# First attention joined in chunks of queries beside its last tiles, with doubled tiles and divided projections, in a two-attention layer on one core

## The chip, the cores and the metric

The kernel runs on one NeuronCore of one Trainium2 chip. The metric is the device time of one execution, in microseconds (us); the median of three runs is what is compared. The profile is one further execution of the same program.

## What is computed

For each of B = 4 sequences of L = 2048 rows of D = 256 values, two attentions follow one another, each with a residual and a layer norm:

```python
# first attention: 16 heads of 16; softmax over m, but the value row is that of the query l
x_proj = (x @ w_in.T + b_in).reshape(b, l, 16, -1);  q, k, v = jnp.split(x_proj, 3, axis=-1)
att = softmax(jnp.einsum('blhd,bmhd->blmh', q, k) * scale, axis=2)
opt = jnp.einsum('blmh,blhd->blhd', att, v).reshape(b, l, d)
x = layernorm(x + opt @ w_out.T + b_out)
# second attention: 4 of 16 heads of 64, chosen by a softmax of the mean of x @ Wr + br
Q, K, V = the chosen heads of x @ Wq + bq, x @ Wk + bk, x @ Wv + bv
O = softmax(Q K^T / 8) V
x = layernorm(x + O @ Wo + bo)
```

## The kernel before

The kernel is one program in which every engine has a list of units of work. A planner, `plan()`, makes the lists when the program is built: it plays the work through with a cost in us for each unit, and writes down in which order each engine took its units. On the chip each engine runs its list strictly in that order and waits on semaphores. So the planner's numbers move no work in time by themselves; they set the order. TensorE (PE) takes the unit with the lowest `spot` among the heads of six hand-made lists (`work_lists()`): `main`, `scores`, `products`, `inputs`, `tiles` and `late`.

The units that matter here, with their names in `plan()`:

- `XT`, `QP`, `KP`, `VP`: transposes of a chunk of 512 rows of x, and its projections to queries, keys and values. `QP` and `KP` take one bank of PSUM each, `VP` two. `LV` splits queries and keys into bf16 levels, `SV` stores them, `LS` loads the levels of one head into `stack`.
- `A`: a tile of the first attention, 128 queries by 1024 keys (two matmuls of 512 columns, two banks). VectorE (DVE) takes the minimum of each row (L1185), ScalarE (ACT) exponentiates and sums (L1003). There are 512 tiles in each sequence: 16 heads by 16 tiles of queries by 2 halves of the keys. PSUM has 8 banks, so at most four tiles are in flight.
- `J`: the halves of the keys are joined. Once all 512 tiles are done, DVE finds the lower minimum for all 16 tiles of queries at once, subtracts (`join_first`), ACT exponentiates, and DVE multiplies, adds, takes the reciprocal and multiplies (`join_second`).
- `AT`, `OT`, `OP`: for each chunk c of 512 queries GpSimd (POOL) scales the value rows (L752), PE transposes them, ACT copies them to `oT`, PE projects them (L830). Then the layer norm: DVE adds the residual and takes the statistics (L1161 to L1171), ACT takes the root (`LN`, L1060 and L1062), and `NM` refines and scales (L712 to L721), on DVE for `OP`.
- `X1`, `RT`, `LW`: the rows are transposed into `x1T` (L838); when all four chunks are there, the routing is worked out on PE, DVE and ACT, and SyncE (SP) loads the weights of the chosen heads.
- `FK`, `FQ`, `FV`: the projections of the second attention (L844, L830). `S`, `T`, `V`: its scores for the maxima (L927, read by DVE L1264), its scores again for the exponentials (L942), and its products (L962). `D`, `R`, `FO`: sums, scaling, output projection and second layer norm.

The sequences overlap: while the second attention of sequence b runs, the tiles `A` of sequence b+1 run between its units. I call the stretch from the last tile `A` of a sequence to the first scores `S` of the same sequence a seam; there are four, and sequence 3 has no tiles of a next one to put into its seam. Before the first seam only sequence 0's tiles run, with all the `inputs` between them (L844, L830 of `fq` and `w_inT`); I call it the first stage. `AHEAD` is the number of tiles of the next sequence that the lists give to a seam.

Of the kernel before, what the change touches and what calls it, by code (L numbers as in the profile page):

```python
# [13 lines left out]
P = 128  # L14
# [3 lines left out]
CH = 512  # L18
# [20 lines left out]
HEAD_TILES = NT * HALF  # L39
RING = 8  # L40
BURST = 4
BURSTS = STEPS // BURST
AHEAD = 20
# [17 lines left out]

def work_lists():
# [4 lines left out]
    main, late, scores, products, inputs, tiles = [], [], [], [], [], []  # L67
# [22 lines left out]
    for b in range(B):  # L90
        if b + 1 < B:
            tiles += place([("A", b + 1, j) for j in range(AHEAD)], b, near)
        first = []
        for c in range(NCH + 2):
            first += [("OT", b, c)] * (c < NCH) + [("OP", b, c - 1)] * (1 <= c <= NCH) + [("X1", b, c - 2)] * (c >= 2)
        first.append(("RT", b))
        first += [("FK", b, 0, c) for c in range(NCH)] + [("FQ", b, 0, 0)]
        main += place(first, b, near)
# [4 lines left out]
    for r in range(B * rounds + behind):  # L103
# [8 lines left out]
        for i, kind in enumerate(spots):  # L112
# [21 lines left out]
            if kind == "V" and at:  # L134
                was = ((at - 1) // GROUPS, (at - 1) % GROUPS)
                main += [(spot, ("D",) + was)] * (step == 4) + [(spot, ("R",) + was)] * (step == 8)
                if at // GROUPS + 1 < B:
                    main += [(spot, ("FO", was[0], was[1] // PAIRS))] * (step == 12 and was[1] % PAIRS == 1)
                else:
                    main += [(spot, ("FO",) + divmod((at - 2) // PAIRS, NCH))] * (step == 2 and at % PAIRS == 1)  # L140
    for b in range(B - 1):
        tiles += [(b + 0.9999, ("A", b + 1, j)) for j in range(given[b], A_TILES)]
    main += [(B + 0.99, ("D", B - 1, GROUPS - 1)), (B + 0.99, ("R", B - 1, GROUPS - 1)), (B + 0.99, ("FO", B - 1, NCH - 1))]
    for units in (late, scores, products, tiles):
        units.sort(key=lambda entry: entry[0])
    main.sort(key=lambda entry: entry[0])
    return [main, scores, products, inputs, tiles, late]


def plan():  # L150
# [9 lines left out]
    def fill(tag, us, banks, after, read_by):  # L160
        name = ("PE",) + tag
        unit(name, us, after)
        banks_of[name], reader[name] = banks, read_by
# [5 lines left out]
    sp = lambda *t: ("SP",) + t  # L169
    jobs = [t for at, t in lists[3] if t[0] == "XT"]  # L170
    norms = []
    for b in range(B):
        norms += [("OP", b, c) for c in range(NCH)] + [("FO", b - 1, NCH - 1)] * (b > 0)
        norms += [("FO", b, c) for c in range(NCH - 1)]
    norms.append(("FO", B - 1, NCH - 1))
# [14 lines left out]
    for i, half in enumerate(halves):  # L190
        for kind, eng in (("QP", dve), ("KP", act)):
            t, two = (kind,) + half, (kind,) + halves[i - 2]
            fill(t, 1.85, 1, [act("XT", half[0], half[2])], eng(*t))
            split = dve if kind == "QP" and half[0] == 0 else pool
            was = dve if kind == "QP" and two[1] == 0 else pool
# [1141 lines left out]
```

## Time and profile before

| | |
|---|---|
| median of 3 runs | 3965.09 us (3962.86 to 3968.43) |
| profiled execution, its own time | 3961.53 us |
| its span | 3959.8 us |
| busy: PE, DVE, ACT, POOL | 90%, 88%, 78%, 41% |
| granted TensorE clock, mean | 0.911 |

The span is the time from the first to the last instruction. A busy share is an average over stages. The granted clock is given as a share of full speed; 1.00 is 2.4 GHz and 0.50 is 1.2 GHz. Views of stretches below show for each engine how long it was busy, and in brackets how many instructions it ran.

### The profile page before, as it was taken

Reading aid. Unit: us, or ns where it says so; the run is one execution under the profiler, and the core shown is the slowest. Engines: PE = TensorE matmul, PEld = TensorE weight load, DVE = VectorE, ACT = ScalarE, POOL = GpSimd, SP = SyncE. Lnnn points to the kernel's source line nnn. Section 1 sums busy time; section 2 is a strip of 40 time slices with the busy share of each in tenths; the row PEclk is TensorE's granted clock in tenths of the full one; section 3 lists DMA queues with packets and bytes.
Section 4 is the critical chain, followed back from the end, with each engine's and each line's share of the span. In section 5 each row is a group of like instructions: output and inputs, shape, how many; then the busy total and the mean of one; then the engine's idle time right before and its main releaser. Section 6 shows DMA issues by size and latency. Waiting matters only on the chain.

```text
span 3959.8 us, 41484 instructions
## 1 busy us (share of the span) xinstructions
PE 3559.1 (90%) x13768; PEld 1260.7 (32%) x13768; DVE 3464.9 (88%) x3484; ACT 3097.4 (78%) x5053; POOL 1624.5 (41%) x1086
## 2 busy tenths in 40 slices
PE   7888888888999999799999999799999999799997
PEld 3233232232223232433322232333323232443333
DVE  7888889979999999879999999879999999667786
ACT  4888888867999999778999999678999999424333
POOL 3122233101444444423444444333444444737675
PEclk7677777679999999899999999799999999899998
DMA  5222222110000000200000000200000000100000
GB/s 161 69 74 71 74 75 73 55 52 17 17 17 27 17 27 17 83 23 12 27 17 27 17 27 16 87 22 17 27 17 27 17 27 1 56 7 12 11 11 11
DMA packets 117192, 142.60 MB, mean 36 GB/s; under 512 B 33394, under 2 KB 100466, under 8 KB 116978
## 3 DMA queue, kind: packets, MB, share of 16 engines
q1 hardware_dynamic: 116978, 139.95, 11.5%
q8 instruction: 110, 1.80, 0.2%
q14 instruction: 104, 0.85, 0.1%
HBM read 89.55 MB, written 50.33 MB: 35 GB/s over the span
## 4 chain that ended last, share of the span: by engine, by line
PE 42%; DVE 39%; ACT 14%; issue 3%; POOL 1%; SPq 1%; DMA 0%; DVEq 0%; POOLq 0%; ACTq 0%
DVE nmax L1185 26%; ACT ps L1003 13%; PE ps L962 10%; DVE smax L1264 9%; PE ps L865 8%; PE ps L830 6%; PE ps L844 6%; PE ps L927 5%; PE ps L942 5%; PE ps L977 1%; PE ps L838 1%; DVE y L721 1%; POOL facc L789 1%; DVE vals L1201 0%; PE ps L945 0%
## 5 line engine op out<-in xcount | busy, mean ns | idle before, releaser
L1003 ACT ACTIVATE ps<-ps,nmax 128x1024 f32<-128x1024 f32 x2048 | 2230.0, 1091 | 302.8 <-DVE nmax L1185 273.5
L1185 DVE TENSOR_REDUCE nmax<-ps 128x1 f32<-128x1024 f32 x2048 | 2382.3, 1215 | 95.3 <-PE ps L865 88.7
L865 PE MATMUL ps<-stack 96*128 96x512 bf16 x4096 | 1342.7, 426 | 206.3 <-ACT ps L1003 122.8
L789 POOL TENSOR_TENSOR facc<-facc,probs 128x1024 f32<-128x1024 f32 x443 | 1041.6, 2351 | 861.0 <-ACT probs L1090 776.4
L865 PEld LDWEIGHTS ps<-stack 96*128 96x128 bf16 x4096 | 280.5, 101 | 1373.9 <-ACT ps L1003 939.7
L1264 DVE TENSOR_REDUCE smax<-ps 128x2 f32<-128x1024 f32 x512 | 619.3, 1215 | 47.1 <-PE ps L927 47.0
L927 PE MATMUL ps<-fk,fq 64*128 64x512 f32 x2048 | 574.5, 644 | 63.1 <-ACT ps L1003 56.8
L942 PE MATMUL ps<-fq,fk 64*128 64x512 f32 x2048 | 548.4, 614 | 10.8 <-DVE probs L1294 5.5
L962 PE MATMUL ps<-probs,vals 128*64 128x512 f32 x2048 | 517.2, 612 | 4.4 <-ACT probs L1090 3.4
L1090 ACT ACTIVATE probs<-ps 128x1024 f32<-128x1024 f32 x384 | 389.2, 1015 | 26.7 <-PE ps L945 26.2
L1003 ACT ACTIVATION_READ_ACCUMULATOR ps<-ps,nmax 128x1 f32 x2048 | 409.0, 200 | 0.0
L1079 ACT ACTIVATE probs<-probs 128x1024 f32<-128x1024 f32 x128 | 135.0, 1056 | 219.3 <-DVE probs L1294 188.4
L942 PEld LDWEIGHTS ps<-fq,fk 64*128 64x128 f32 x2048 | 190.1, 190 | 289.9 <-issue 139.8
L927 PEld LDWEIGHTS ps<-fk,fq 64*128 64x128 f32 x2048 | 165.2, 187 | 301.4 <-ACT ps L1003 201.0
L699 POOL CAST fk<-vals 128x512 bf16<-128x512 f32 x56 | 35.3, 631 | 458.8 <-DVE vals L1191 368.4
L962 PEld LDWEIGHTS ps<-probs,vals 128*64 128x64 f32 x2048 | 116.8, 136 | 267.6 <-issue 205.8
L795 POOL TENSOR_TENSOR oacc<-oacc,part 128x512 f32<-128x512 f32 x72 | 90.8, 1262 | 259.4 <-ACT part L1100 259.4
L1294 DVE TENSOR_TENSOR probs<-ps,stack 128x1024 f32<-128x1024 f32 x128 | 154.7, 1215 | 37.5 <-PE ps L942 28.6
L786 POOL TENSOR_TENSOR facc<-probs 128x1024 f32<-128x1024 f32 x32 | 75.2, 2349 | 266.5 <-ACT probs L1090 227.5
L945 PE MATMUL ps<-frows,minus 64*128 64x512 bf16 x768 | 149.2, 382 | 0.0
L844 PE MATMUL ps<-fq,w_inT 128*128 128x512 f32 x256 | 136.1, 663 | 9.6 <-ACT fq L1009 4.8
L844 PE MATMUL ps<-x1T,wqk_sel 128*128 128x512 f32 x256 | 128.2, 637 | 12.9 <-DMA bqk_sel<-in_L_ffn_bq 10.2
(127 smaller groups left out, 2035.6 us busy)
## 6 DMA issues: line engine op xcount, KB each, us to landing
stack<-qk_levels SPq DMA_DIRECT2D x768, 64.0 KB, 2.2
qk_levels<-fk SPq DMA_DIRECT2D x64, 384.0 KB, 2.6
probs<-in_L_attn_x SPq DMA_DIRECT2D x16, 512.0 KB, 3.8
res<-in_L_attn_x SPq DMA_DIRECT2D x16, 512.0 KB, 4.4
v_rows<-vals SPq DMA_DIRECT2D x16, 512.0 KB, 2.6
vrows<-v_rows SPq DMA_DIRECT2D x16, 512.0 KB, 3.4
x_rows<-y SPq DMA_DIRECT2D x16, 512.0 KB, 2.9
res<-x_rows SPq DMA_DIRECT2D x16, 512.0 KB, 3.8
```

The lines of the kernel that those rows point to most:

```text
L789: pool.tensor_tensor(total, total, probs[:, slot, :], ALU.add).then_inc(facc_ready, 1)
L830: last = pe.matmul(ps[:, banks[t // 2], (t % 2) * D:(t % 2 + 1) * D], rowsT[:, cc, t * P:(t + 1) * P], w[:, cc, :], start=(cc == 0), stop= ...
L844: last = pe.matmul(bank(banks[0]), wT(cc), columns(cc), start=(cc == 0), stop=(cc == KC - 1))
L865: last = pe.matmul(bank(banks[i]), stack[0:SK, hd % 2, 0, t * P:(t + 1) * P], stack[0:SK, hd % 2, 1, col:col + CH], start=True, stop=True)
L927: last = pe.matmul(bank(banks[h]), fq[rows, pair, qs:qs + P], fk[rows, pair, ks:ks + CH], start=True, stop=True)
L942: last = pe.matmul(bank(banks[h]), fk[rows, pair, s * P:(s + 1) * P], fq[rows, pair, c * CH:(c + 1) * CH], start=True, stop=b + 1 == B)
L962: last = pe.matmul(ps[rows, into, :], vals[:, s, (2 * pair + h) * FD:(2 * pair + h + 1) * FD], probs[:, slot_of(b, g, s), h * CH:(h + 1) * ...
L1003: act.activation(src, src, ACT.Exp, bias=nmax[:, b % 2, half, t, hd:hd + 1], scale=-1.0, accum_out=esum[:, b % 2, half, t, hd:hd + 1]).the ...
L1090: act.activation(probs[:, slot_of(b, g, s), :].rearrange("p (h n) -> p h n", h=2), two_banks(banks), ACT.Exp, scale=float(FD) ** -0.5).the ...
L1185: dve.tensor_reduce(nmax[:, b % 2, half, t, hd:hd + 1], two_banks(banks), AX.XY, ALU.min).then_inc(min_ready, 1)
L1264: dve.tensor_reduce(smax[:, g % 2, s // NCH, :, s % NCH], two_banks(banks), AX.X, ALU.max).then_inc(smax_ready, 1)
L1294: dve.tensor_tensor(probs[:, slot_of(b, g, s), :].rearrange("p (h n) -> p h n", h=2), two_banks(banks), bc[:, g % 2, :].rearrange("p (h n) ...
```

## The change

1. **Joining by chunks.** `CHUNK_LAST` names the last tile of each chunk of 512 queries in the last head (every 8th of its 32 tiles). For each chunk, as soon as its tiles are done, DVE takes the lower minimum (128x64), POOL subtracts (128x128), ACT exponentiates, POOL multiplies and adds, DVE takes the reciprocal, and POOL multiplies before it scales the value rows. `nmax` and `att` hold the values, no longer `oT`. A new list `seam` holds `OT`, `OP`, `X1`, `RT` and the first `FK` and `FQ`, with spots from the tiles of their chunks.
2. **Layer norm.** `NM` of `OP` goes to POOL for the first three chunks (`nm`), and stays on DVE for the last. The order of the norms changes with it.
3. **`AHEAD`** is 32 in place of 20.
4. **Divided projections** (`PARTS`): `QP`, `KP`, `FK`, `FQ` and `D` are issued in two pieces, `VP`, `FV`, `OP` and `FO` in four, and other units can come between the pieces. The banks are held from the first piece. By `PATIENT` a tile goes ahead of such a piece when the planner has nothing queued on DVE.
5. **Doubled tiles** (`again`): where the planner has work queued on DVE and none of the last 12 PE units was `S`, `T`, `BC` or `V`, the two matmuls of a tile are issued twice, with the same operands into the same banks. 324 of the 512 tiles of sequence 0 are doubled, and 17, 15 and 15 of the others.
6. **Splitting.** `LV` of the queries of sequence 0's second half of heads goes from DVE to POOL (4 of 8 on DVE go).
7. **Planner.** The cost of `A` on PE is 0.47 in place of 0.437, of `A` and `S` on DVE 1.165 in place of 1.135. Units in `URGENT` go first on an engine.

```diff
+CHUNK_LAST = [A_TILES - HEAD_TILES + (c + 1) * TPC * HALF - 1 for c in range(NCH)]
-AHEAD = 20
+AHEAD = 32
+PARTS = {"QP": 2, "KP": 2, "FK": 2, "FQ": 2, "VP": 4, "FV": 4, "OP": 4, "FO": 4, "D": 2}
+URGENT = ("J", "AT", "OT", "OP", "X1", "RT")
+PATIENT = {k: 20 for k in ("QP", "KP", "VP", "XT", "FK", "FQ", "FV", "OP", "FO", "OT", "X1", "D", "R", "RT")}
+NEAR = 12
...
+    nm = lambda k, b, c: ((dve if k == "OP" and c + 1 == NCH or k == "FO" and b + 1 == B else pool)("NM", k, b, c))
...
-        unit(dve("J", b, 0), 1.2, [act("A", b, A_TILES - 1)] + ([pe("FO", b - 2, NCH - 1)] if b >= 2 else []))
-        unit(act("J", b), 0.63, [dve("J", b, 0)])
-        unit(dve("J", b, 1), 4.2, [act("J", b)])
         for c in range(NCH):
-            unit(pool("AT", b, c), 1.95, [dve("J", b, 1), sp("LV", b, c)])
+            unit(dve("J", b, c, 0), 0.6, [act("A", b, CHUNK_LAST[c])] + ([pool("AT", b - 1, c)] if b else []))
+            unit(pool("J", b, c, 0), 0.4, [dve("J", b, c, 0)])
+            unit(act("J", b, c), 0.4, [pool("J", b, c, 0)])
+            unit(pool("J", b, c, 1), 0.6, [act("J", b, c)])
+            unit(dve("J", b, c, 1), 0.5, [pool("J", b, c, 1)])
+            unit(pool("AT", b, c), 2.2, [dve("J", b, c, 1), sp("LV", b, c)])
...
+            kind = best and best[2][3 if best[2][1] == "part" else 1]
+            if not queued and kind in PATIENT and at[4] < len(tiles):
+                spot, t = tiles[at[4]]
+                if pe(*t) in pe_ready and pick(2) and spot < best[0] + PATIENT[kind] / A_TILES:
+                    best = (spot, 4, pe(*t))
...
+                twice = n[1] == "A" and queued and not any(m[1] in mode for m in order["PE"][-NEAR:])
+                if twice:
+                    again.add(n)
...
+                elif kind == "J":
+                    b, c, later = at
+                    both, whole = of_chunk(c, nmax[:, b % 2, :, :, :]), chunk_att(c)
+                    base = (b * NCH + c) * COMB_STEPS
+                    if later == 0:
+                        pool.wait_ge(lowest, b * NCH + c + 1)
+                        pool.tensor_tensor(both, whole.unsqueeze(1).to_broadcast([P, HALF, TPC * AH]), both,
+                                           ALU.subtract).then_inc(comb, 1)
+                    else:
+                        pool.wait_ge(comb_e, b * NCH + c + 1)
+                        pool.tensor_tensor(both, both, of_chunk(c, esum[:, b % 2, :, :, :]), ALU.mult).then_inc(comb, 1)
+                        pool.wait_ge(comb, base + 2)
+                        pool.tensor_tensor(whole, both[:, 0, :], both[:, 1, :], ALU.add).then_inc(comb, 1)
...
-                    for i in range(2):
+                    for i in (0, 1, 0, 1) if n in again else (0, 1):
```

The first place is PE in the middle of the first stage, where the chunks of sequence 1 are projected; `stack` marks matmuls of tiles, `w_inT,fq` the value projection `VP`, `fq,w_inT` the query and key projections, `ident,probs` the transposes `XT`. Before:

```order
L865 MATMUL ps<-stack 128x512 x34
L830 MATMUL ps<-w_inT,fq 128x256 x8
L865 MATMUL ps<-stack 128x512 x10
L838 MATMUL ps<-ident,probs 128x128 x8
L865 MATMUL ps<-stack 128x512 x12
L844 MATMUL ps<-fq,w_inT 128x512 x2
```

The same place in the changed kernel:

```order
L932 MATMUL ps<-stack 128x512 x46
L892 MATMUL ps<-w_inT,fq 128x256 x4
L932 MATMUL ps<-stack 128x512 x4
L892 MATMUL ps<-w_inT,fq 128x256 x2
L932 MATMUL ps<-stack 128x512 x2
L892 MATMUL ps<-w_inT,fq 128x256 x2
L932 MATMUL ps<-stack 128x512 x6
L901 MATMUL ps<-ident,probs 128x128 x8
```

The value projection stood in one piece and now has two and then one tile between its pieces, and the run of tiles ahead of it has more matmuls because most of its tiles are doubled.

The second place is DVE at the end of sequence 1's tiles. `nmax<-ps` are its minima of tiles, `smax` those of the second attention's scores, and `oT` holds the joined values. Before:

```order
L1132 TENSOR_TENSOR oT<-nmax 128x256
L1134 TENSOR_TENSOR oT<-oT,nmax 128x512
L1264 TENSOR_REDUCE smax<-ps 128x2
L1141 TENSOR_TENSOR oT<-oT,esum 128x512
L1143 TENSOR_TENSOR oT<-oT 128x256
L1145 RECIPROCAL oT<-oT 128x256
L1148 TENSOR_TENSOR att<-oT 128x256
```

In the changed kernel the first two chunks there:

```order
L1258 TENSOR_TENSOR att<-nmax 128x64
L1231 TENSOR_REDUCE nmax<-ps 128x1 x2
L1320 TENSOR_REDUCE smax<-ps 128x2
L1231 TENSOR_REDUCE nmax<-ps 128x1 x2
L1261 RECIPROCAL nmax<-att 128x64
L1231 TENSOR_REDUCE nmax<-ps 128x1 x6
L1258 TENSOR_TENSOR att<-nmax 128x64
L1231 TENSOR_REDUCE nmax<-ps 128x1
L1320 TENSOR_REDUCE smax<-ps 128x2
L1231 TENSOR_REDUCE nmax<-ps 128x1
L1261 RECIPROCAL nmax<-att 128x64
L1231 TENSOR_REDUCE nmax<-ps 128x1 x4
```

DVE's six instructions on all the queries have become two small ones for each chunk, with 3 to 5 minima between them, in which POOL and ACT must have done their parts.

The third place is POOL at the last chunk of sequence 1; `facc` are the running sums of the second attention, `newt`, `rstd` and `y` are `NM`, `res` is the residual with its bias, `vrows` is `AT`. Before, POOL's part of the whole join was:

```order
L789 TENSOR_TENSOR facc<-facc,probs 128x1024 x4
L752 TENSOR_TENSOR vrows<-vrows,att 128x1024 x4
L771 CAST flevels<-fmax 128x8
```

In the changed kernel, for the last chunk:

```order
L796 TENSOR_TENSOR nmax<-att,nmax 128x2x64
L848 TENSOR_TENSOR facc<-facc,probs 128x1024
L800 TENSOR_TENSOR nmax<-nmax,esum 128x2x64
L802 TENSOR_TENSOR att<-nmax 128x64
L749 TENSOR_TENSOR newt<-rstd 128x4
L751 TENSOR_TENSOR newt<-newt,var 128x4
L753 TENSOR_SCALAR newt<-newt 128x4
L755 TENSOR_TENSOR rstd<-rstd,newt 128x4
L758 TENSOR_SCALAR y<-y,mv,rstd 128x256 x4
L818 TENSOR_TENSOR res<-res,b_out_rows 128x1024
L807 TENSOR_TENSOR att<-att,nmax 128x64
L811 TENSOR_TENSOR vrows<-vrows,att 128x1024
```

One `facc` addition stands between the two parts of the join, and the scaling of another chunk's norm and a residual stand between the join and `AT`.

## Rows read from the trace of the kernel before

**Rows 1.** The page: span, and each engine's busy time

```profile
span 3959.8 us, 41484 instructions
PE 3559.1 (90%) x13768; PEld 1260.7 (32%) x13768; DVE 3464.9 (88%) x3484; ACT 3097.4 (78%) x5053; POOL 1624.5 (41%) x1086
```

**Rows 2.** Stages: length, busy time of each engine, granted clock, DMA share, GB/s

```profile
59.00:757.00 698.00, 603.00 (x1547) 192.91 (x1546) 624.00 (x559) 601.32 (x1064) 174.81 (x200) 0.71 0.22 72
757.00:957.00 200.00, 158.45 (x535) 70.03 (x534) 163.63 (x210) 134.06 (x233) 24.49 (x15) 0.81 0.15 46
957.00:1606.00 649.00, 606.76 (x2528) 185.91 (x2529) 620.59 (x570) 603.26 (x989) 282.16 (x169) 0.98 0.07 20
1606.00:1806.00 200.00, 168.77 (x670) 75.92 (x668) 156.68 (x207) 139.49 (x231) 73.02 (x47) 0.88 0.17 52
2484.00:2684.00 200.00, 167.88 (x668) 75.21 (x664) 157.49 (x207) 139.49 (x232) 72.76 (x47) 0.89 0.17 51
3367.00:3478.00 111.00, 86.96 (x384) 46.65 (x382) 59.77 (x106) 48.94 (x72) 73.01 (x44) 0.86 0.19 56
3478.00:3960.00 482.00, 451.47 (x1964) 183.95 (x1960) 358.10 (x379) 168.43 (x176) 295.99 (x167) 0.97 0.03 9
```

**Rows 3.** DVE's waits in the first stage: us in total, times, longest

```profile
DVE vals L1201 <- PE ps L830: 44.5, 14, 4.4
DVE vals L1191 <- PE ps L844: 19.5, 20, 2.3
```

**Rows 4.** Timeline of the first stage: start, length, engine, line, count

```profile
400.39 3.72 PE L844 MATMUL ps<-fq,w_inT 128*128 128x512 f32 x4
...
406.96 1.88 PE L844 MATMUL ps<-fq,w_inT 128*128 128x512 f32 x4
...
739.62 18.18 DVE L1185 TENSOR_REDUCE nmax<-ps 128x1 f32<-128x1024 f32 x16
```

**Rows 5.** A 10 us window of the first stage, columns as in rows 2

```profile
730.00:740.00 10.00, 9.13 (x19) 1.18 (x18) 10.00 (x10) 10.00 (x19) 0.00 (x0) 0.50 0.00 0
```

**Rows 6.** DVE's timeline in the seam of sequence 1, idle time ahead in brackets

```profile
1606.28 2.27 DVE L1132 TENSOR_TENSOR oT<-nmax 128x256 f32<-128x256 f32 x1
...
1613.08 2.52 DVE L1143 TENSOR_TENSOR oT<-oT 128x256 f32<-128x256 f32 x1
...
1617.42 0.42 DVE L1148 TENSOR_TENSOR att<-oT 128x256 f32<-128x256 f32 x1
...
1639.01 3.42 DVE L721 TENSOR_SCALAR y<-y,mv,rstd 128x256 f32<-128x256 f32 x4
...
1704.87 0.75 DVE L1246 TENSOR_SCALAR fq<-ps,bqk_sel 128x512 f32<-128x512 f32 x1 [10.20 <-PE ps L844]
...
1707.80 1.22 DVE L1264 TENSOR_REDUCE smax<-ps 128x2 f32<-128x1024 f32 x1
```

**Rows 7.** The same seam until the first scores, and after, columns as in rows 2

```profile
1606.00:1708.00 102.00, 75.38 (x276) 40.15 (x272) 78.89 (x138) 65.22 (x114) 33.87 (x25) 0.77 0.28 87
1708.00:1806.00 98.00, 93.39 (x396) 35.78 (x396) 77.79 (x70) 74.27 (x118) 39.14 (x22) 1.00 0.06 15
```

**Rows 8.** Minima of tiles alone in that seam: DVE busy, clock, DMA, GB/s

```profile
1606.00:1708.00 102.00, 37.22 (x32) 0.77 0.28 87
```

**Rows 9.** The chain through that seam: start, length, what ran

```profile
1694.48 10.35 PE ps L844 x20
...
1705.05 0.86 PE ps L865 x4
```

**Rows 10.** Groups by shape: busy us, mean ns, idle ahead

```profile
L721 POOL TENSOR_SCALAR y<-y,mv,rstd 128x256 f32<-128x256 f32 x48 | 58.0, 1221 | 1.3
...
L721 DVE TENSOR_SCALAR y<-y,mv,rstd 128x256 f32<-128x256 f32 x80 | 42.4, 593 | 0.7
...
L1164 DVE BATCH_NORM_STATS2 st<-y 128x6 f32<-128x256 f32 x128 | 45.0, 414 | 1.1
...
L752 POOL TENSOR_TENSOR vrows<-vrows,att 128x1024 f32<-128x1024 f32 x16 | 30.4, 1932 | 82.1 <-DVE att L1148 82.1
```

More of the change, by code:

```diff
@@ L142, in work_lists @@
         tiles += [(b + 0.9999, ("A", b + 1, j)) for j in range(given[b], A_TILES)]
+    spot_a = {t[1:]: spot for spot, t in tiles}
+    for b in range(B):
+        done = [spot_a[b, j] for j in CHUNK_LAST]
+        seam += [(done[c], (kind, b, c)) for c, kind in ((0, "OT"), (0, "OP"), (0, "X1"), (1, "OT"), (1, "OP"))]
+        seam += [(done[c], (kind, b, c)) for c, kind in ((2, "OT"), (2, "OP"), (1, "X1"))]
+        rest = [("OT", b, 3), ("OP", b, 3), ("X1", b, 2), ("X1", b, 3), ("RT", b)]
+        rest += [("FK", b, 0, c) for c in range(NCH)] + [("FQ", b, 0, 0)]
+        seam += place(rest, max(b, done[3]), near)
     main += [(B + 0.99, ("D", B - 1, GROUPS - 1)), (B + 0.99, ("R", B - 1, GROUPS - 1)), (B + 0.99, ("FO", B - 1, NCH - 1))]
-    for units in (late, scores, products, tiles):
+    for units in (main, late, scores, products, tiles):
         units.sort(key=lambda entry: entry[0])
-    main.sort(key=lambda entry: entry[0])
-    return [main, scores, products, inputs, tiles, late]
+    for units in (main, late, inputs, seam):
+        whole, units[:] = list(units), []
+        for spot, t in whole:
+            parts = PARTS.get(t[0], 1)
+            units += [(spot + i * GAP / A_TILES, ("part", i) + t if i + 1 < parts else t) for i in range(parts)]
+    return [main, scores, products, inputs, tiles, late, seam]
 def plan():
@@ L160, in fill @@
     def fill(tag, us, banks, after, read_by):
-        name = ("PE",) + tag
-        unit(name, us, after)
-        banks_of[name], reader[name] = banks, read_by
+        parts = PARTS.get(tag[0], 1)
+        for i in range(parts):
+            name = ("PE",) + (("part", i) if i + 1 < parts else ()) + tag
+            unit(name, us / parts, after if i == 0 else [])
+            banks_of[name] = banks if i == 0 else 0
+            if i == 0:
+                reader[name] = read_by
     pe = lambda *t: ("PE",) + t
@@ L332, in arrive @@
         else:
-            ready[n[0]].append((now, rank[n], n))
+            ready[n[0]].append((n[1] not in URGENT and n[2] != "OP", now, rank[n], n))
             queued += n[0] == "DVE"
@@ L369, in plan @@
                     held[n] = pick(banks_of[n])
+                    held[n[:1] + n[3:] if n[1] == "part" else n] = held[n]
                     free.difference_update(held[n])
@@ L530, in build @@
         NEWTON_STEPS = 4
-        COMB_STEPS = 6
+        COMB_STEPS = 3
         ROUTE_STEPS = 11
         QK_DMAS, V_DMAS = 4 * FH // PAIRS, 2 * FH
-        order, held, freed, planned = plan()
-        fill_no = {n[1:]: i + 1 for i, n in enumerate(n for n in order["PE"] if n in held and n[1] != "V")}
+        order, held, freed, again, planned = plan()
+        fill_no = {n[1:]: i + 1 for i, n in enumerate(n for n in order["PE"] if n in held and n[1] not in ("V", "part"))}
         nth = {}
@@ L824, in _, with pieces, project_rows @@
             pe.wait_ge(wT_read, 3)
-            def project_rows(banks, rowsT, w):
-                for t in range(TPC):
+            def pieces(kind, piece, count):
+                parts = PARTS.get(kind, 1)
+                return range(count * piece // parts, count * (piece + 1) // parts)
+            def project_rows(kind, piece, banks, rowsT, w):
+                for t in pieces(kind, piece, TPC):
                     for cc in range(KC):
@@ L973, in _ @@
                             shares = (g % 2,)
-                        for t in range(TPC):
+                        for t in pieces(kind, piece, TPC):
                             for h in range(2):
```

143 lines of the change are left out of this document (71 added, 72 removed).

## The prediction

> **What bounds the kernel now.** I read the page's busy shares first [rows 1]: PE 90%, DVE 88%, ACT 78% of the span. No engine is full, so the question is where DVE and PE stand idle. The stages tell it [rows 2]. Between two seams (957 to 1606 us) DVE is busy 620.6 of 649 us and PE 606.8 at a clock of 0.98: nothing is to be had there but less work. The idle time lies in three places. In the first stage (59 to 757) DVE is busy 624.0 of 698.0, 74.0 idle, at a clock of 0.71. In the seams and what follows them it is idle 36.4, 43.3 and 42.5 us of 200 each (the seam of sequence 1 stands for 0 and 2, which differ little), and in the last seam (3367 to 3478) PE, which bounds everything after it, is idle 24.0 of 111.0. The last stage (3478 to 3960) is PE's: 451.5 of 482.0. There the change alters nothing that I price.
>
> Why DVE idles in the first stage is in its waits [rows 3]: 44.5 us for the value projection, 14 times, and 19.5 us for query projections, 20 times: 64.0 of the 74.0. The timeline shows why it is so long [rows 4]: the four matmuls of a projection take 3.72 us where the clock is low and 1.88 where it is high. A tile costs DVE 18.18 / 16 = 1.136 us, so the at most three tiles that wait in PSUM feed it for 3.4 us; a value projection is twice as long as a query projection and outlasts them. Tiles alone leave the clock at its lower level: 0.50, with DVE at 10.00 of 10.00 [rows 5]. So a low clock costs nothing by itself there, only at the projections.
>
> **The change part by part.**
>
> *Divided projections, first stage.* A quarter of a value projection is about 1.9 us at the low clock (3.72 / 2), half a query projection the same, and two tiles then come between pieces. That is under the 3.4 us in PSUM, so the waits should mostly go. But the first two pieces often stand together (the first place shown), 3.7 us. Bounds: 20 us, if only a third of the waits goes, and 64, all of them. I take three quarters, 48.
>
> *Doubled tiles, first stage.* A tile's two matmuls take 0.43 us at the high clock (0.86 for four [rows 9]), a doubled tile 0.86: under 1.136, so DVE sees nothing. At half the clock a doubled tile takes 1.72 and PE paces DVE: 0.58 lost for each. A single tile at the low clock (0.86) costs nothing. The gain of doubling is only that the projections meet a high clock, which the dividing has already made harmless. No row shows what the clock does under doubled tiles. It stood at 0.98 between the seams, where tiles and the second attention share PE [rows 2], and at 0.50 in the tiles alone [rows 5]; doubled tiles are nearer to the former in what they give PE to do. I charge a few dips, 14 tiles' worth: 8 us. Bounds 0 and 324 x 0.58 = 188. First stage: 48 - 8 = **40**. The splitting moved to POOL goes from before the first tile, while PE and the load of the stack are awaited too: nothing, at most 2.
>
> *The seam of sequence 1.* From 1606 to the first scores at 1707.8 it takes 102 us, in which DVE is busy 78.9 [rows 6, 7], 37.2 of it with 32 tiles of the next sequence [rows 8]. In the changed order 42 such tiles stand there: 42 x 1.136 = 47.7. Of the other 41.7 us these go: the join, 10.4 by rows 6 and its neighbours (12 us until 1617.84, less one score reduction of 1.2); three scalings of 4 x 593 ns [rows 10], 7.1; and the statistics of two norms, which now come before the last tile, 4 x 414 ns and an addition of 1.2 each, 5.7. What comes: two small join instructions, each under the 0.42 of L1148 [rows 6], 0.8, and two more score reductions, 2.4. So 41.7 - 10.4 - 7.1 - 5.7 + 0.8 + 2.4 = 21.7, with the tiles 69.4 us for DVE.
>
> Is the chain that short? Before, the join takes 12 us, then 77 us pass for four chunks, routing and loads until PE starts the projections at 1694.5 [rows 9], then 10.4, and 3 to the scores. Now only the last chunk is left. For POOL it is small join instructions (by L752's rate 0.24 for 128x128; I take 0.4 each with their start, 1.6), one scaling of another chunk ahead of `AT`, 4 x 1.22 = 4.9 [rows 10], an addition and a residual of at least 1.9 each, and `AT` 1.9: about 12, no less than the old join. Then one chunk, routing and loads, for which I take 45 of the 77, and projections with tiles between, 15: 72. With the hops in which each step queues behind a tile I take 78 for the seam.
>
> The gain, with tiles counted as work that leaves another stage: before 102 - 37.2 = 64.8; now 78 - 47.7 = 30.3, and 5.7 for the work moved ahead of the last tile (5.7 + three chunks' join 2.4 - the reductions moved in 2.4): 64.8 - 30.3 - 5.7 = 28.8. After the first scores DVE idles another 20.2 of 98.0 us beside PE at 93.4 [rows 7]; the divided `FV` and `FK` give back perhaps 4, since PE has only 4.6 to give. Against it stand two new waits. DVE's `J` minimum has two inputs in SBUF; such instructions took 2.27 and 2.52 us where L1148 took 0.42 [rows 6], beside POOL's additions: up to 2.1 for each of four chunks; I take 3 in all. And DVE's reciprocal of each chunk waits for a round trip over POOL, ACT and POOL; behind it, strictly in order, stand the minima of tiles, for which ACT and then PE wait. Only 3 to 5 minima cover it (3.4 to 5.7 us), and on POOL an addition of sums stands between the two join parts. I take 0.8 a chunk, 3 in all. The 15 doubled tiles cost PE 15 x 0.43 = 6.5 where it is idle anyway: 1. So 28.8 + 4 - 3 - 3 - 1 = 25.8, **26** for each of three seams, **78**. On SP the loads of the next head's stack keep their place behind the weights, except in the first seam, where one load of 12 goes ahead of them while the chain is elsewhere: nothing. Bounds for a seam: 0, and all its idle time, 36.4, 43.3 and 42.5, 122 in all.
>
> *The last seam.* No tiles fill it, so the chain sets it and PE's idle time can go: 24.0, and some at the clock of 0.86. Bounds 0 and 31; I take **18**, since the same two waits stand here.
>
> A rule speaks to the moved scaling. The row: 1221 ns on POOL against 593 on DVE, the latter with its waits in it [rows 10]. The Trainium skill, GPSIMD Engine Reference, Engine selection, says that work with one input runs on GpSimd at roughly line rate. By it the scaling ahead of `AT` would take 2.4 instead of 4.9 us, and the sum would be 2.5 larger for each of four seams, 10 us; the trace decides for the longer.
>
> **The sum.** 40 + 78 + 18 = 136. The profiled execution took 3961.5, which lies 3.6 below the median of 3965.1. 3961.5 - 136 = 3825.5; with the 3.6, **3829 us**.
>
> **The rivals.**
>
> *The seams close wholly* (0.15). DVE's order holds enough tiles, and the idle time of all stages goes: 60 + 110 + 28 = 198, so 3767. For it: 69.4 us of work against 102. Against it: PE follows the seam at 93.4 of 98.
>
> *The seams are no shorter* (0.12). POOL's list is the mechanism: its join parts stand behind additions of sums that wait for ACT's exponentials, and `AT` of the last chunk behind a residual's load. Then each seam gives 3 and the last none: 40 + 9 = 49, 3916. For it: POOL 33.9 of 102 busy leaves room, but strictly in order. Against: three of four chunks are out of the chain in any case.
>
> *The doubled tiles keep PE at the low clock* (0.07), the other side. Its place is the first stage; its price 0.58 for each doubled tile that runs at 0.50. Above (136 + 8) / 0.58 = 248 of 324 such tiles, the kernel is slower: with all, 188, it comes to 3829 - 8 + 188 = 4009. Half of them: 3915. For it: tiles alone fell to 0.50 [rows 5]. Against: PE would then have no gap at all, and the last stage, where it is busy nearly throughout, had 0.97 [rows 2].
>
> *The change does nothing* (0.03): DVE sets the time, the clock stays, 3965.
>
> My forecast has the rest, 0.63, with its own range from 3790 to 3875: the first stage between 20 and 64, a seam between 15 and 38.
>
> **How the numbers follow.** The range from 3772 to 3900 takes the forecast's, and the upper part of the seams that close, and leaves out most of the last three rivals, about 0.2. A measurement here can tell 0.2% (8 us) from no change. Faster: 0.63 + 0.15 + 0.12 and part of the clock's case, 0.91; same 0.03; slower 0.06.
>
> **What would show it.** The first stage should be about 658 us long and DVE's waits for L892 and L907 under 20 us; the clock there above 0.85 if doubling works, and near 0.6 with PE at 100% if it does not. From the last tile to the first scores of sequences 0 to 2 about 78 us with some 42 to 50 tiles in them; in the last seam about 90 of 111. DVE's reciprocal should wait under 1 us on average. I am wrong if the first stage grows, if DVE's idle time in the seams goes to the reciprocals' waits, or if the stages between the seams, which I leave alone, grow by what the seams lose, since PE there is at 93%.

## The result and the profile after

The changed kernel takes 3876.62 us (median of 4 runs, 3868.99 to 3883.73) against 3966.09 us for the kernel before (4 runs). The ratio is 0.9777 with a 95% interval from 0.9764 to 0.9790: 89 us, or 2.2%, less. The forecast was 3829 us, 136 less, with a range from 3772 to 3900. The profiled execution took 3876.35 us.

The page of the changed kernel, span, busy time and granted clock by slices:

```profile
span 3874.3 us, 43074 instructions
...
PE 3551.2 (92%) x14510; PEld 1298.5 (34%) x14510; DVE 3414.4 (88%) x3380; ACT 3102.1 (80%) x5065; POOL 1729.0 (45%) x1262
...
PEclk9999999899999999899999999899999999999998
```

Its stages, cut at the end of a sequence's last tile and at its first scores; [rows 2] and [rows 7] are cut within 3 us of the same events of the kernel before. They are in order: the first stage; the seam of sequence 0; the stage up to the last tile of sequence 1; the seam of sequence 1, the 100 us after it and the rest up to the last tile of sequence 2; the whole from one last tile to the next, which I call a period; the last seam; the last stage.

```profile
57.40:703.70 646.30, 589.27 (x2231) 226.34 (x2230) 623.34 (x567) 602.30 (x1069) 200.83 (x233) 0.99 0.25 81
703.70:792.30 88.60, 73.98 (x258) 32.85 (x258) 74.62 (x108) 76.86 (x141) 23.86 (x26) 0.83 0.28 81
892.30:1552.50 660.20, 608.81 (x2528) 194.89 (x2528) 620.37 (x580) 594.94 (x973) 299.26 (x191) 0.97 0.08 22
1552.50:1637.40 84.90, 77.74 (x308) 38.20 (x309) 68.48 (x103) 70.93 (x126) 39.38 (x43) 0.85 0.29 85
1637.40:1737.40 100.00, 96.69 (x413) 36.67 (x410) 84.50 (x75) 80.93 (x130) 39.93 (x23) 1.00 0.03 8
1737.40:2426.20 688.80, 634.44 (x2649) 208.11 (x2647) 646.11 (x609) 615.57 (x1005) 314.64 (x204) 0.98 0.08 24
1552.50:2426.20 873.70, 808.87 (x3364) 282.98 (x3364) 799.10 (x786) 767.43 (x1259) 393.95 (x269) 0.97 0.10 28
3300.00:3388.10 88.10, 74.79 (x336) 35.41 (x336) 28.07 (x61) 43.06 (x62) 71.50 (x58) 0.93 0.18 53
3388.10:3874.30 486.20, 459.29 (x1980) 183.12 (x1976) 356.69 (x379) 169.17 (x177) 304.97 (x171) 0.97 0.03 9
```

The same period of the kernel before, and its part from 100 us after the first scores:

```profile
1603.70:2481.20 877.50, 801.46 (x3334) 276.72 (x3332) 803.53 (x808) 765.44 (x1256) 371.49 (x229) 0.97 0.10 28
1807.80:2481.20 673.40, 628.73 (x2646) 199.41 (x2648) 643.06 (x600) 622.35 (x1020) 297.22 (x181) 0.99 0.07 21
```

The reader is to see where the 89 us are. All times in this paragraph are between the same two events. The first stage, from the first tile's minimum to the last tile, went from 695.4 us (59.0 to 754.4) to 646.3, its clock from 0.71 to 0.99, and DVE is idle 23.0 us of it. The seam of sequence 1 went from 104 us (1603.7 to 1707.8) to 85, and the last from 115 (3364.1 to 3478.8) to 88. But this period is only 3.8 us shorter: what the seam and the 100 us after it gave, the rest took back, 688.8 us where it was 673.4. DVE's idle time in it is 74.6 us, where it was 74.0. In the kernel before this rest held some 430 tiles by the trace, now 417, so it grew although work had left it. The period before it went from 849.3 to 848.8 us and the one after it from 882.9 to 873.8. The three seams at the head of these periods are 52 us shorter in all, the periods 13: a quarter.

DVE's waits in such a period, kernel before (us in total, times, the longest):

```profile
DVE nmax L1185 <- PE ps L865: 27.6, 61, 3.8
DVE fq L1246 <- PE ps L844: 13.2, 7, 10.2
```

and the changed kernel:

```profile
DVE nmax L1231 <- PE ps L932: 56.7, 100, 3.2
DVE smax L1320 <- PE ps L994: 8.4, 17, 1.0
```

The long wait of the seam (10.2 us for a query projection) is gone; in its place 39 more tiles come late, 29 us in all.

### The profile page after: what moved, and what is told of

Read it like the earlier page. It is cut to its first block, busy times and chain, and to the rows that moved or that the text cites. A ratio compares the mean times of both kernels' runs of the same rounds, so it can differ in the third digit from the quotient of the medians.

```text
span 3874.3 us, 43074 instructions
## 1 busy us (share of the span) xinstructions
PE 3551.2 (92%) x14510; PEld 1298.5 (34%) x14510; DVE 3414.4 (88%) x3380; ACT 3102.1 (80%) x5065; POOL 1729.0 (45%) x1262
## 4 chain that ended last, share of the span: by engine, by line
PE 44%; DVE 33%; ACT 17%; issue 5%; POOL 1%; DMA 0%; SPq 0%; DVEq 0%; POOLq 0%; ACTq 0%
DVE nmax L1231 21%; ACT ps L1071 14%; PE ps L1029 10%; PE ps L932 9%; DVE smax L1320 7%; PE ps L994 7%; PE ps L1009 7%; PE ps L892 5%; PE ps L907 4%; PE ps L1044 1%; PE ps L1012 1%; DVE st L1208 1%; PE ps L901 1%; ACT part L1171 1%; ACT probs L1161 1%
## 5 line engine op out<-in xcount | busy, mean ns | idle before, releaser
L932 PE MATMUL ps<-stack 96*128 96x512 bf16 x4838 | 1369.4, 391 | 192.4 <-ACT ps L1071 104.3
L932 PEld LDWEIGHTS ps<-stack 96*128 96x128 bf16 x4838 | 355.7, 99 | 1324.0 <-ACT ps L1071 757.8
L1009 PE MATMUL ps<-fq,fk 64*128 64x512 f32 x2048 | 557.7, 624 | 16.4 <-DVE probs L1350 5.4
L1071 ACT ACTIVATION_READ_ACCUMULATOR ps<-ps,nmax 128x1 f32 x2048 | 421.4, 206 | 0.0
L736 POOL CAST fk<-vals 128x512 bf16<-128x512 f32 x60 | 37.6, 627 | 393.7 <-DVE vals L1237 346.5
L1350 DVE TENSOR_TENSOR probs<-ps,stack 128x1024 f32<-128x1024 f32 x128 | 154.6, 1216 | 39.5 <-PE ps L1009 20.2
L907 PE MATMUL ps<-x1T,wqk_sel 128*128 128x512 f32 x256 | 132.7, 618 | 6.7 <-DMA bqk_sel<-in_L_ffn_bq 3.6
L907 PE MATMUL ps<-fq,w_inT 128*128 128x512 f32 x256 | 128.7, 614 | 6.7 <-ACT fq L1077 4.8
```

The source lines that it names most:

```text
L907: last = pe.matmul(bank(banks[0]), wT(cc), columns(cc), start=(cc == 0), stop=(cc == KC - 1))
L932: last = pe.matmul(bank(banks[i]), stack[0:SK, hd % 2, 0, t * P:(t + 1) * P], stack[0:SK, hd % 2, 1, col:col + CH], start=True, stop=True)
L1009: last = pe.matmul(bank(banks[h]), fk[rows, pair, s * P:(s + 1) * P], fq[rows, pair, c * CH:(c + 1) * CH], start=True, stop=b + 1 == B)
L1071: act.activation(src, src, ACT.Exp, bias=nmax[:, b % 2, half, t, hd:hd + 1], scale=-1.0, accum_out=esum[:, b % 2, half, t, hd:hd + 1]).the ...
```

## The experiments

All kernels are variants of the changed kernel, whose ratio is 0.9777. Times of the first stage come from one profiled execution each.

**Join at the end.**

```diff
-CHUNK_LAST = [A_TILES - HEAD_TILES + (c + 1) * TPC * HALF - 1 for c in range(NCH)]
+CHUNK_LAST = [A_TILES - 1] * NCH
...
-unit(dve("J", b, c, 0), 0.6, [act("A", b, CHUNK_LAST[c])] + ([pool("AT", b - 1, c)] if b else []))
+unit(dve("J", b, c, 0), 0.6, [act("A", b, CHUNK_LAST[c])] + ([pool("AT", b - 1, c)] if b else []) + ([dve("J", b, c - 1, 1)] if c else []))
```

The order of the norms is the old one here.

> The changed kernel with one part undone: all four chunks' joins wait for the sequence's last tile and follow one another, so no chunk's join, transposes or projections stand ahead of it; doubling, dividing and POOL's share stay. Theory A (the join by chunks is worth what I gave it, and other edits take some of it back in the stages between the seams): it loses what the seams gave, 3 x 26 + 18, so 95 to 100 us more than the changed kernel, a ratio to the kernel before near 1.002. Theory B (the stretch between two last tiles is bound by what PE and DVE have to do in all of it, and a shorter seam only moves idle time): it loses 3 x 4 and some 20 in the last seam, 30 to 40 us, a ratio near 0.986.

3908.12 us, ratio 0.9866 (0.9843 to 0.9890): by the ratios 35 us more than the changed kernel, the sum that theory B had. Its seam of sequence 1, the period that it begins, and its last sequence from the last tile to the end:

```profile
1533.80:1651.00 117.20, 97.46 (x391) 47.30 (x390) 97.02 (x142) 94.08 (x165) 59.56 (x67) 0.85 0.28 84
1533.80:2417.50 883.70, 812.54 (x3372) 285.45 (x3370) 798.87 (x786) 767.56 (x1258) 394.39 (x268) 0.96 0.10 28
...
3298.30:3909.70 611.40, 549.70 (x2363) 228.65 (x2361) 407.55 (x467) 220.78 (x254) 396.39 (x252) 0.94 0.06 18
```

Joining by chunks shortens this seam by 117.2 - 84.9 = 32 us and this period by 10. The next period is 7 us shorter for it, 873.8 and 880.8. But the one before is 12 longer, 848.8 and 836.7, and so is the first stage by 8, 646.3 and 638.5, since with the join at the end no chunk's projections stand ahead of the last tile. Up to the last tile of sequence 3 the two kernels take the same time (3300.0 and 3298.3 us). All of the 35 us comes behind that tile, where no tiles follow: 611.4 - 574.3 = 37. So theory B's sum came, but not its parts. Nor is this the join of the kernel before: here four joins follow one another over DVE, POOL and ACT, and the last seam takes 127.5 us where the kernel before had 114.7. Against the kernel before, the time behind the last tile is 21 us shorter.

**The two remedies of the first stage, one and both undone.** Single tiles:

```diff
-twice = n[1] == "A" and queued and not any(m[1] in mode for m in order["PE"][-NEAR:])
+twice = False
```

> The changed kernel without doubled tiles (371 of them single again), all else as changed. By my prediction the dividing alone makes a low clock harmless: the clock of the first stage falls back to 0.6 to 0.8, the stage stays at 646 us or is up to 8 us shorter, ratio 0.976 to 0.978. Rival (what the first stage gained comes from the clock that the doubled tiles hold up): the first stage is 20 to 40 us longer, ratio 0.983 to 0.988.

Whole input projections (`QP`, `KP` and `VP` left out of `PARTS`):

```diff
-PARTS = {"QP": 2, "KP": 2, "FK": 2, "FQ": 2, "VP": 4, "FV": 4, "OP": 4, "FO": 4, "D": 2}
+PARTS = {"FK": 2, "FQ": 2, "FV": 4, "OP": 4, "FO": 4, "D": 2}
```

> The changed kernel with the input projections (query, key, value of the first attention) in one piece again, the tiles doubled. If the doubled tiles hold the clock up, a value projection takes half as long as before and lasts about as long as the three waiting tiles feed DVE: the first stage loses 5 to 15 us of its 49, ratio 0.979 to 0.982. Rival (only short pieces free DVE): it loses 30 or more, ratio above 0.985.

and both edits together:

> The changed kernel with the input projections whole and all tiles single: both remedies of the first stage undone, the rest as changed. Both theories: the first stage goes back to about 695 us, ratio 0.989 to 0.991, clock there 0.6 to 0.8. Beside the two kernels that lack one of them it tells how far the two overlap.

| kernel | median, us | ratio (95%) | first stage, us |
|---|---|---|---|
| changed | 3876.62 | 0.9777 (0.9764 to 0.9790) | 646.3 |
| whole inputs | 3904.76 | 0.9864 (0.9835 to 0.9893) | 672.5 |
| single tiles | 3950.57 (10 runs) | 0.9972 (0.9961 to 0.9984) | 698.4 |
| both undone | 3987.01 | 1.0070 (1.0043 to 1.0096) | 735.5 |

The first stage with single tiles, at a clock of 0.76:

```profile
57.00:755.00 698.00, 584.95 (x1579) 195.97 (x1578) 622.96 (x566) 602.65 (x1069) 200.99 (x234) 0.76 0.24 74
```

and with doubled tiles and whole inputs, at 0.99:

```profile
58.00:731.00 673.00, 593.76 (x2250) 229.65 (x2248) 624.20 (x567) 606.11 (x1071) 200.89 (x233) 0.99 0.24 77
```

Times the ratios' differences by 3966, doubling is worth 77 us with divided inputs and 82 with whole ones, dividing 34 and 39. They add up; neither makes the other harmless. The first stages alone show less of it, 52 and 63 us for doubling, 26 and 37 for dividing. The profiled executions of two of these kernels were the fastest of theirs, 3933.96 us with single tiles and 3893.19 with whole inputs, so those two stages may be short by some us. With single tiles my theory failed, and the rival was right in its direction and too small (20 to 40 us). With whole inputs the ratio is the rival's, the stage's 26 us lie between the two. With both undone the stage is 40 us longer than both theories had it. The place that shows why, at a value projection, in the kernel with single tiles; PE, then DVE:

```profile
411.46 7.60 PE L932 MATMUL ps<-stack 96*128 96x512 bf16 x14 [0.49 <-ACT ps L1071]
419.12 3.78 PE L892 MATMUL ps<-w_inT,fq 128*128 128x256 f32 x8
422.70 1.91 PE L932 MATMUL ps<-stack 96*128 96x512 bf16 x4
...
423.80 3.48 DVE L1231 TENSOR_REDUCE nmax<-ps 128x1 f32<-128x1024 f32 x3 [2.76 <-PE ps L932]
```

and the same place in the changed kernel:

```profile
382.87 12.57 PE L932 MATMUL ps<-stack 96*128 96x512 bf16 x46 [0.32 <-ACT ps L1071]
395.49 1.99 PE L892 MATMUL ps<-w_inT,fq 128*128 128x256 f32 x8
397.32 1.03 PE L932 MATMUL ps<-stack 96*128 96x512 bf16 x4
...
397.95 3.49 DVE L1231 TENSOR_REDUCE nmax<-ps 128x1 f32<-128x1024 f32 x3 [0.55 <-PE ps L932]
```

A tile matmul takes 7.60 / 14 = 0.54 us in the one and 12.57 / 46 = 0.27 in the other. Two quarters of the value projection that stand together, with two tiles behind them, take 5.7 us at the low clock and 3.0 at the high one, and three minima cover 3.4. The granted clock was 0.53 in the one (419 to 425 us) and 1.00 in the other (395 to 399). DVE waits 2.76 us and 0.55. Over the whole first stage DVE waits 74.0 us in the kernel with single tiles:

```profile
DVE nmax L1231 <- PE ps L932: 44.5, 30, 2.9
DVE vals L1237 <- PE ps L907: 29.5, 12, 2.6
```

In the changed kernel it waits 22.2 (shown further below). The difference, 51.8 us, is the 52.1 us between the two stages.

**The rule that puts tiles first, and the planner's costs.** Single tiles again; first without the rule of `PATIENT` in the first stage, then with whole inputs too:

```diff
-if not queued and kind in PATIENT and at[4] < len(tiles):
+if not queued and kind in PATIENT and at[4] < len(tiles) and tiles[at[4]][1][1] > 0:
```

> The changed kernel with all tiles single, input projections divided, and in the first stage without the planner's rule that lets a tile go ahead of a projection whose place has come while nothing queues for DVE. Single tiles with that rule gave a first stage of 698 us. Theory A (the rule bunches projections and banks, and spoils what dividing gains at a low clock): the first stage comes to 650 to 665 us, as my sum had it for dividing alone, ratio 0.983 to 0.988. Theory B (at a low clock PE has no room for pieces between tiles, rule or not): 690 to 710 us, ratio 0.996 to 1.000.

> As the run before this one, but with the input projections whole too: single tiles, whole input projections, no such rule in the first stage, so that this stage differs from the kernel before only by POOL's share of the splitting and the planner's costs. Theory A (the rule made the undone first stage 40 us longer than before): about 695 us, ratio 0.994 to 0.997. Theory B (the costs or POOL's share did it): 725 to 740, ratio 1.003 to 1.008.

The first came to 3941.12 us, ratio 0.9930 (0.9913 to 0.9946), its first stage to 726.5; the second to 3974.38 us (10 runs), 1.0016 (1.0002 to 1.0029), its first stage to 749.9. So the rule did not lengthen the first stage: without it this stage is 28 and 14 us longer in the profiled executions, and the later stages are shorter by 25 and 12. The medians are 9 and 13 us lower, by the ratios 17 and 21: with single tiles the kernel does better without the rule. Theory A fell both times, and both stages were longer than theory B's too (up to 710 and 740 us). The costs were next, on top of the second of these kernels:

```diff
-fill(("A", b, j), 0.47, 2, ...
+fill(("A", b, j), 0.437, 2, ...
-unit(dve("A", b, j), 1.165, ...
+unit(dve("A", b, j), 1.135, ...
-unit(dve("S", *t), 1.165, ...
+unit(dve("S", *t), 1.135, ...
```

> Single tiles, whole input projections, no tile-first rule in the first stage, as in the run whose first stage took 749.9 us, and now the planner's old costs of tiles too. They put the projections of the first stage back into the close order of the kernel before (one value projection, then QP, 2 tiles, KP, 1 tile, QP, 2 tiles, KP, 17 tiles, where the new costs have 6, 1, 10 and 5 tiles between them). Theory A (that order was worth the 54 us by which the undone first stage is longer than before's): 690 to 705 us, ratio 0.988 to 0.991. Theory B (the splitting moved to POOL or the engines' new order of urgency did it): above 735, ratio 0.999 or more.

3933.89 us, 0.9902 (0.9876 to 0.9928): 45 us less by the ratios, of which the first stage gave 32 (717.4). The ratio is theory A's; the stage lies between the two theories. The new costs spread the projections, and with single tiles that is dear. This stage is still 22 us longer than in the kernel before, but the period behind it is 23 us shorter (825.9 and 849.3). So work of the chunks has moved ahead of the last tile; the seam behind that tile is 78 us long, where it was 103. That this is all of the 22 us is not shown: POOL's share of the splitting is in all these kernels and was not tried alone.

The same costs in the changed kernel, with doubled tiles:

> The changed kernel with the planner's costs of tiles and score reductions as before (0.437 and 1.135 instead of 0.47 and 1.165); the program is otherwise the same. If the costs made the stages between the seams longer (DVE's idle time there 42.6 us instead of 30.3), each gets 8 to 12 us shorter, ratio 0.968 to 0.972. Rival (they only shuffle the order): within 5 us in all, ratio 0.976 to 0.979.

3871.97 us, 0.9759 (0.9742 to 0.9776): the first stage 638.2, the period 870.6, 3 less than with the new costs. The median is 5 us below the changed kernel's, and the two intervals overlap. The costs are not what lengthened the stages between the seams; this is the rival's result. The change has one more part that its list does not name: `D`, `R` and `FO` stand at steps 3, 6 and 9 of a group, where they stood at 4, 8 and 12. With `D` and `R` at steps 4 and 8 as well:

```diff
-(step == 3) + [(spot, ("R",) + was)] * (step == 6)
+(step == 4) + [(spot, ("R",) + was)] * (step == 8)
```

> The changed kernel with the planner's old costs of tiles and score reductions, as in the run that came out 5 us faster than the changed kernel, and with D and R back at steps 4 and 8 of a group. If the earlier steps 3 and 6 are part of what the stages between the seams lost, a period gets 3 to 8 us shorter than with the old costs alone, ratio 0.968 to 0.973, and it is the fastest of all; rival (they cost nothing): 0.975 to 0.977, as with the old costs alone.

3867.84 us (3859.23 to 3882.84), 0.9736 (0.9711 to 0.9761). Its profiled execution was the slowest of its four, with a period of 877.3, so the profile doesn't show the gain that I expected there. It is the fastest median of the kernels that leave nothing out, some 9 us below the changed kernel. Its interval overlaps that of the old costs alone, so neither the theory nor its rival is shown.

**Whole pieces in the seam and between.** `FK`, `FQ`, `FV`, `FO` and `D` in one piece:

```diff
-PARTS = {"QP": 2, "KP": 2, "FK": 2, "FQ": 2, "VP": 4, "FV": 4, "OP": 4, "FO": 4, "D": 2}
+PARTS = {"QP": 2, "KP": 2, "VP": 4, "OP": 4}
```

> The changed kernel with the second attention's projections and denominators (FK, FQ, FV, FO, D) in one piece again; the inputs and OP stay divided. If the pieces, which hold their banks from the first to the last with tiles between, make tiles late in the stages between the seams (DVE waits for them 56.7 us in a period instead of 27.6), those stages get 8 to 12 us shorter and the seams some 4 longer, ratio 0.970 to 0.974. Rival (whole pieces cost DVE more than the banks do): the periods grow by 5 to 15 us each, ratio 0.981 to 0.989.

3884.78 us, 0.9790 (0.9770 to 0.9810), 5 us more, with the two intervals overlapping. Its period is 88.6 + 100 + 684.9 = 873.5, the changed kernel's 873.7. Neither theory holds. In the whole kernel DVE waits 33.2 us for `FV` and 68.6 for the output projections, and 7.3 and 45.1 where they are divided, but the time does not follow these waits. On the other side, its DVE has 8 us less work in this period (790.97), so two effects may cancel here. That the banks held by the pieces cost nothing is not shown.

**What bounds a period.** DVE lightened (the score maxima over half the columns), then PE (three quarters of the score columns):

```diff
-dve.tensor_reduce(smax[...], two_banks(banks), AX.X,
+dve.tensor_reduce(smax[...], two_banks(banks)[:, :, 0:CH // 2], AX.X,
```

> The changed kernel with DVE's work lightened between the seams, to see what bounds it there: the row maxima of the second attention's scores are taken over half the columns only (that part of the computation is left out), about 0.55 us less for each of 128 reductions of a sequence, 70 us of the 874 from one last tile to the next; PE's work is untouched. If DVE paces these stages, a period gets 60 us or more shorter; if PE does, under 15; if both share it, as DVE's idle time that stayed at 74 us a period suggests, 25 to 45. The last sequence's stage is PE's and does not move. Ratio 0.93 if DVE's, 0.967 or more if PE's, 0.945 to 0.96 if shared.

```diff
-last = pe.matmul(bank(banks[h]), fq[rows, pair, qs:qs + P], fk[rows, pair, ks:ks + CH],
+last = pe.matmul(bank(banks[h])[:, 0:3 * P], fq[rows, pair, qs:qs + P], fk[rows, pair, ks:ks + 3 * P],
```

> The mirror of the run before: the score matmuls of the second attention write 384 of 512 columns (the rest is left out), a quarter of the 306 us that they take of PE in a period, some 75; DVE's work is untouched. If PE paces the stages between the seams, a period gets 60 us shorter or more, if DVE does, under 15, and if both share it 25 to 45. The last stage gets 50 to 75 shorter in any case. Should the granted clock in these stages fall with PE's work (it stands at 0.97), the gain says less, and I read it with the clock. Ratio 0.915 if PE's, 0.955 if DVE's, near 0.935 if shared.

3820.02 us, 0.9624 (0.9601 to 0.9646), and 3851.61 us, 0.9705 (0.9682 to 0.9728). Groups of the changed kernel in 800 us between seams (mean ns behind the busy us):

```profile
L1320 DVE TENSOR_REDUCE smax<-ps 128x2 f32<-128x1024 f32 x121 | 146.9, 1216 | 8.7 <-PE ps L994 8.4
...
L994 PE MATMUL ps<-fk,fq 64*128 64x512 f32 x486 | 139.9, 653 | 10.8 <-ACT ps L1071 8.9 <-DVE smax L1320 1.5 <-DVE fq L1302 0.3
```

The group with light DVE, and then that kernel's period:

```profile
L1320 DVE TENSOR_REDUCE smax<-ps 128x2 f32<-128x512 f32 x125 | 85.1, 684 | 15.8 <-PE ps L994 15.7
```

```profile
1532.20:2388.70 856.50, 798.46 (x3362) 276.75 (x3361) 734.69 (x785) 763.71 (x1259) 393.90 (x269) 0.98 0.10 29
```

The group with light PE, and then that kernel's period:

```profile
L994 PE MATMUL ps<-fk,fq 64*128 64x384 f32 x496 | 116.0, 545 | 11.6 <-ACT ps L1071 9.7 <-DVE smax L1320 1.5 <-DVE fq L1302 0.3
```

```profile
1547.90:2418.50 870.60, 788.44 (x3363) 281.90 (x3363) 797.14 (x785) 768.20 (x1259) 394.17 (x269) 0.97 0.10 28
```

128 maxima, each 0.53 us shorter, are 68 us of DVE's time; the period gets 17.2 shorter, a quarter of it (the other two 22.0 and 13.7). That is less than the 25 of a shared bound and more than the 15 of a bound by PE. The run with light PE is a smaller test than I meant. I had counted on 75 us less for PE, from durations that overlap; its busy time falls by 20.4 us, and the period by 3.1, about a sixth (the other two 4.4 and 3.3). The last stage, from which I expected 50 to 75, gave 15 (470.8 for 486.2). Had either engine paced the period alone, its 68 or 20 us would have come out whole; neither did. The clock, 0.97 and 0.98, did not interfere. ACT is busy 767.43 of 873.70 us and is the engine that gives tiles their banks back; I have not lightened it, so what takes the rest is open.

## Why the prediction was partly right

The forecast was 136 us less, and 89 came. The time, 3876.62 us, lies in the range up to 3900, but just above the range from 3790 to 3875 that the forecast had for itself. The direction was right and the first stage and the last seam gave near what was said, the former by luck; the 78 us for three seams were 13.

**The first stage.** I gave it 40 us and it gave some 49, but the step that I built it on failed: "The gain of doubling is only that the projections meet a high clock, which the dividing has already made harmless". Doubling gives 52 us of the first stage (77 of the kernel) and not -8, dividing 26 of the stage with doubled tiles and 37 with single ones (34 and 39 of the kernel), and not 48. That the two sum to more than the stage gained is the third error: I put the planner's new costs at nothing, without a reason, and with single tiles and whole inputs they cost 45 us, with the changed kernel's remedies 5. The term was right in size by errors that cancel, which is luck. What I overlooked stood in my own text: two quarters often stand together, 3.7 us at the low clock, and the tile behind them takes another 0.9 before DVE gets it. I had the number and compared 3.7 with 3.4 as if the excess were all. That "a low clock costs nothing by itself there" fits the tiles alone [rows 5]; the first pieces after them pay, and the tile behind these. The signs named were met: clock above 0.85 (0.99), waits for projections under 20 us (8.2 for L907, none listed for L892). In the changed kernel's first stage:

```profile
DVE nmax L1231 <- PE ps L932: 14.0, 28, 1.2
DVE vals L1237 <- PE ps L907: 8.2, 12, 0.7
```

The rival of a low clock under doubled tiles is refuted; the stage's clock is 0.99.

**The seams of sequences 0 to 2.** The signs inside the seam came near what I said: 78 us forecast, 84.9 measured (88.6 and 85.0 the other two), 42 tiles in it, DVE's reciprocals with next to no wait. The 100 us behind it gave the 4 us, 20.2 idle before and 15.5 now. DVE's work in the seam was said to be 69.4 us and is 68.48. What failed is the sum "28.8 + 4 - 3 - 3 - 1 = 25.8", of which the three periods gave 0.5, 3.8 and 9.1. The join alone gave -12, 10 and 7 by the kernel without it. I valued each microsecond that leaves the seam at one microsecond of time, with tiles "counted as work that leaves another stage". The lightened DVE puts the rate at a quarter: 17.2 for 68. And less work left DVE than I counted: busy 803.53 before, 799.10 after, 4.4 us, where 10.4 + 7.1 - 0.8 = 16.7 were counted on. 6 us of the missing 12 went into one kind of instruction, the addition of epsilon to the variances, and 4 into the join's own, 5.0 us in place of 0.8. Before and after, in a period:

```profile
L1171 DVE TENSOR_SCALAR var<-mv 128x4 f32<-128x4 f32 x8 | 3.8, 479 | 0.3
```

```profile
L1215 DVE TENSOR_SCALAR var<-mv 128x4 f32<-128x4 f32 x8 | 10.0, 1253 | 0.3
...
L1258 DVE TENSOR_TENSOR att<-nmax 128x64 f32<-128x64 f32 x4 | 2.8, 707 | 2.0 <-ACT ps L1071 2.0
L1261 DVE RECIPROCAL nmax<-att 128x64 f32<-128x64 f32 x4 | 2.2, 540 | 0.0
```

I had feared this for the join's minimum and charged 3 us; it struck the variances more. What holds them is shown in the last section. The last sign that I named for being wrong, that "the stages between the seams, which I leave alone, grow by what the seams lose", describes what happened. Its reason, PE at 93%, is not borne out: PE with 20 us less to do frees 3.

**The last seam.** 18 forecast. From the last tile to the end it took 3959.8 - 3364.1 = 595.7 us before and 574.3 now, 21 less, with a last seam that is 27 shorter. Here the chain sets the time, and a shorter chain is worth most of what it loses.

**POOL's scalings.** The Trainium skill (GPSIMD Engine Reference, Engine selection) has one-input work at roughly line rate on GpSimd. For this scaling the rows disagree, before [rows 10] and after: 1219 ns on POOL against 408 on DVE for 128x256. Not all one-input work is slow there: POOL's cast of 128x512 (L736) took 627 ns. No run puts these scalings back on DVE, so their price in time is not shown.

```profile
L758 POOL TENSOR_SCALAR y<-y,mv,rstd 128x256 f32<-128x256 f32 x96 | 115.8, 1219 | 2.5
...
L758 DVE TENSOR_SCALAR y<-y,mv,rstd 128x256 f32<-128x256 f32 x4 | 1.4, 408 | 0.0
```

**The sum** of the two profiled executions: up to the last tile of sequence 0 51 us (754.4 before, 703.7 after), from there to the last tile of sequence 3 13 us (to 3364.1 and 3300.0), behind it 21: 85 of 3959.8 - 3874.3 = 85.5. "The seams are no shorter" (3916) had its reason wrong, since they are shorter, but its price for them, 3 each, was nearer to the measured 13 in all than my 26 each. The list `AHEAD`, POOL's scalings and its share of the splitting were tried in no run alone, so how the 13 us divide among them and the join is open.

## What to carry to other kernels

In this kernel, whose engines are about 90% busy, shortening one stretch of a period moved most of its idle time into the next stretch. Judge such an edit by the time from one period's mark to the next, over all periods, since one of three can mislead (-12, 10 and 7 us for the join). Find the rate by lightening an engine before pricing an edit on it: here 0.25 us for each us of DVE, and some 0.8 for each us of the seam only in the tail, where nothing fills in (21 of 27). When two remedies aim at the same wait, do not let one cancel the other on paper: the last sum to check is pieces that stand together, plus the first tile behind them, at the low clock. A planner's costs are an edit like any other: a change of 3 to 8% in them was worth 45 us in one setting, and in another 5, which is hardly clear of the noise.

## What the runs showed of the hardware

Matmuls that compute nothing new keep the granted clock up: 324 doubled tiles raised it from 0.76 to 0.99 over 640 us, and PE still waited for ACT's banks between them. DVE's addition of epsilon, on 128x4 numbers, took from 170 to 1997 ns in one period. The trace shows what holds it: an instruction of POOL with two inputs that has already begun. Once held and once free:

```profile
1147.88 4.82 POOL L848 TENSOR_TENSOR facc<-facc,probs 128x1024 f32<-128x1024 f32 x2 [8.41 <-ACT probs L1161]
...
1148.26 1.99 DVE L1215 TENSOR_SCALAR var<-mv 128x4 f32<-128x4 f32 x1
...
1559.77 0.17 DVE L1215 TENSOR_SCALAR var<-mv 128x4 f32<-128x4 f32 x1
1559.91 2.35 POOL L848 TENSOR_TENSOR facc<-facc,probs 128x1024 f32<-128x1024 f32 x1 [0.71 <-ACT probs L1161]
```

In the first case the first of POOL's two additions runs 2.34 us, until 1150.22, and DVE's instruction ends at 1150.25. Of the 32 such instructions of the changed kernel, 17 begin while a two-input instruction of POOL of over 1 us is running (`facc`, `res`, `vrows`), and of the 32 of the kernel before, 7. All 24 end 0.02 to 0.03 us after POOL's does; the other 40 took 169 to 246 ns. POOL's one-input scalings (L758) held none. That the changed order brings the two together more often costs DVE 6 us a period; no run takes this away by itself.
